# Windowed cross-attention on Trainium2: the projections of the next batch moved behind the attention of the older one

## What is computed

```python
def _L0_xattn_ref(x, cond, Wq, bq, Wk, bk, Wv, bv, Wo, bo):
    H, W = 8, 16                                  # heads, window
    q = Wq @ x + bq; k = Wk @ cond + bk; v = Wv @ cond + bv   # [128, 1024] per batch
    k, v = (pad(t, left=8, right=7) for t in (k, v))
    k_win, v_win = (t[:, :, arange(T)[:, None] + arange(W)[None, :]] for t in (k, v))
    dots = einsum('bhdt,bhdtw->bhtw', qh, k_win) * hd ** -0.5
    out = einsum('bhtw,bhdtw->bhdt', softmax(dots), v_win)
    return Wo @ out + bo
...
x = x + tanh(g_xattn[0]) * _L0_xattn_ref(_layernorm(x), ctx_4096, ...)
```

## Time and profile before

| what | value |
|---|---|
| median of 3 runs | 3655.55 us (3651.84 to 3661.02) |
| the profiled execution | 3649.41 us, span 3647.7 us |
| PE busy | 3294.2 us (90%) |
| DVE busy | 1433.3 us (39%) |
| ACT busy | 889.8 us (24%) |
| mean granted TensorE clock | 0.954 of full speed |

### The profile page before, as it was taken

The page is one execution under the profiler, slowest core; times in us unless marked ns, Lnnn a source line. Parts: engine busy times, 40 slices in busy tenths (PEclk is TensorE's granted clock), DMA queues, the critical chain, the costliest instruction groups (busy, mean ns, idle before and its releaser), DMA issues. The chain is left out here.

```text
span 3647.7 us, 52611 instructions
## 1 busy us (share of the span) xinstructions
PE 3294.2 (90%) x21047; PEld 2507.2 (69%) x21076; DVE 1433.3 (39%) x2021; ACT 889.8 (24%) x1232; POOL 349.3 (10%) x304
## 2 busy tenths in 40 slices
PE   5888855999799997899999669999999999999999
PEld 2454442777678885566666458888888888778777
DVE  6666657777220002677676362111121122310000
ACT  1222243333121112555454221111111111200000
POOL 2000000000000001232222111111111111000000
PEclk9999977999789998999999879999999999999999
DMA  4656451221232223121121243222222222544443
GB/s 95 131 115 126 89 185 35 70 70 59 76 104 69 61 60 110 70 85 58 64 80 63 66 131 103 91 94 94 94 94 94 94 94 82 202 145 132 141 141 104
DMA packets 339441, 352.61 MB, mean 97 GB/s; under 512 B 154352, under 2 KB 261472, under 8 KB 337264
## 3 DMA queue, kind: packets, MB, share of 16 engines
q1 hardware_dynamic: 339312, 350.79, 31.1%
HBM read 215.23 MB, written 126.97 MB: 94 GB/s over the span
## 5 line engine op out<-in xcount | busy, mean ns | idle before, releaser
L2213 PE MATMUL g_ps<-g_xs,g_wt 128*128 128x512 f32 x4128 | 957.2, 392 | 0.0
L2213 PEld LDWEIGHTS g_ps<-g_xs,g_wt 128*128 128x128 f32 x4128 | 774.3, 189 | 160.7
L2269 PE MATMUL g_ps<-g_wd,g_h 128*128 128x512 f32 x2016 | 463.0, 392 | 6.8 <-DMA g_h<-g_hidden 4.1
L2269 PEld LDWEIGHTS g_ps<-g_wd,g_h 128*128 128x128 f32 x2016 | 381.1, 189 | 88.1 <-DMA g_h<-g_hidden 4.7
L2131 DVE SCALAR_TENSOR_TENSOR g_act_out<-g_ps,g_g,g_act_out 128x512 f32<-128x512 f32 (+1 forms) x88 | 66.1, 751 | 691.4 <-ACT g_act_out L2063 691.4
L2063 ACT ACTIVATE g_act_out<-g_ps 128x512 f32<-128x512 f32 (+1 forms) x88 | 52.6, 598 | 655.7 <-PE g_ps L2213 655.7
L1263 PE MATMUL kv_gps<-kv_xh,kv_wh 128*128 128x512 f32 x512 | 200.5, 392 | 0.0
L1263 PE MATMUL kv_gps<-kv_xl,kv_wh 128*128 128x512 f32 x512 | 199.3, 389 | 0.0
L1263 PE MATMUL kv_gps<-kv_xh,kv_wl 128*128 128x512 f32 x512 | 199.3, 389 | 0.0
L1008 PE MATMUL f_gps<-f_xt,f_qwh 128*128 128x256 f32 x1024 | 194.2, 290 | 1.4 <-DVE f_xt L887 1.4
L1611 PEld LDWEIGHTS a_tps<-a_ident,a_e 128*128 128x128 f32 x1024 | 113.4, 144 | 104.6 <-issue 90.5
(11 more groups left out here) (247 smaller groups left out, 4257.6 us busy)
## 6 DMA issues: line engine op xcount, KB each, us to landing
g_h<-g_hidden SPq DMA_DIRECT2D x176, 256.0 KB, 2.6
g_hidden<-g_h SPq DMA_DIRECT2D x84, 512.0 KB, 2.7
kv<-kv_y SPq DMA_DIRECT2D x16, 1024.0 KB, 5.7
a_kv<-kv SPq DMA_DIRECT2D x16, 1024.0 KB, 4.9
g_xb<-x SPq DMA_DIRECT2D x24, 512.0 KB, 4.0
g_down<-g_raw SPq DMA_DIRECT2D x22, 512.0 KB, 2.8
g_raw<-g_down SPq DMA_DIRECT2D x22, 512.0 KB, 4.3
g_raw<-in_L_ffn_gate_w_dram SPq DMA_DIRECT2D x21, 512.0 KB, 4.0
```

The source lines that it names most:

```text
L2213: w = pe.matmul(gps[:, c % 2, m, :], wt[m][i][:, l, ks], xs[c][:, r, k, :], start=(k == 0 and a == 0), stop=(k == NK - 1 and a == 2))
L2269: w = pe.matmul(to, tile[:, p % RING, l, cols], wd[f][:, r, os], start=(f == 0 and a == 0), stop=False)
```

## The change

Five things are altered, in `window_attention` only.

1. x has five places instead of four, and its load is issued one batch earlier.
2. PE's order: the two key halves are projected first, alternating with `scores`; the attend loop has no values in it; the two query halves come between the last `attend` and the transposes of `output(b)`; the two value halves come between those transposes and the product with Wo, which is now `final(b)`.
3. The second half of the queries and of the values goes to a bank of the score ring instead of `prj` (`half_bank`), and the waits are changed to match.
4. ACT: keys first, queries after the last `middle`, the copy of `o` before the exponential. DVE: `normalize(b)` between the maximum and the subtraction, `value` halves around `sums`.
5. SP: `spread_keys` before `store_values`.

```diff
@@ -62,10 +62,11 @@
     RING = 3
+    XS = 5

         s = Scope(nc, ctx, "w")
-        x = s.sb("x", [P, 4, D])
+        x = s.sb("x", [P, XS, D])
         cond = s.sb("cond", [P, 2, D])
...
@@ -121,11 +122,15 @@

+        def half_bank(n, i, a):
+
+            return prj[:, :] if a == 0 or i == 1 else sps[:, (NK * n + i // 2) % RING, :]
+
         @block.sync
             def load_x(n):
-                past(sp, "res", n - 3)
-                sp.dma_start(x[:, n % 4, :], x_in[n]).then_inc(xl[n % 4], 16)
+                past(sp, "res", n - XS + 1)
+                sp.dma_start(x[:, n % XS, :], x_in[n]).then_inc(xl[n % XS], 16)

...
@@ -179,13 +185,13 @@
                     store(b - 1)
-                    if there(b + 3):
-                        load_x(b + 3)
+                    if there(b + 4):
+                        load_x(b + 4)
                 if b >= -1 and there(b + 3):
                 if there(b + 2):
+                    spread_keys(b + 2)
                     store_values(b + 2)
-                    spread_keys(b + 2)
                     spread_values(b + 2)
...
@@ -244,7 +250,7 @@
                 past(act, "s", NK * (n - 1))
-                act.activation(q[n % 2][:, 512 * a:512 * a + 512], prj[:, :], ACT.Identity, bias=bias[:, 0:1]).then_inc(S["sbq"], 1)
+                act.activation(q[n % 2][:, 512 * a:512 * a + 512], half_bank(n, 0, a), ACT.Identity, bias=bias[:, 0:1]).then_inc(S["sbq"], 1)

...
@@ -260,27 +266,28 @@
             for b in range(-2, B):
-                for i in range(4):
-                    if there(b + 2):
-                        (query, key)[i // 2](b + 2, i % 2)
+                for t in range(NK):
+                    if there(b + 2) and t < 2:
+                        key(b + 2, t)
                     if there(b + 1):
-                        middle(b + 1, i)
-                if there(b + 1):
-                    for t in range(4, NK):
                         middle(b + 1, t)
-                    act.wait_ge(S["sub"], b + 2)
-                    act.activation(sc[:, :, :, :], sc[:, :, :, :], ACT.Exp, scale=SCALE).then_inc(S["ex"], 1)
+                if there(b + 2):
+                    for a in range(2):
+                        query(b + 2, a)
                 if there(b):
                     act.copy(o[:, :], tps[:, :]).then_inc(S["oe"], 1)
+                if there(b + 1):
+                    act.wait_ge(S["sub"], b + 2)
+                    act.activation(sc[:, :, :, :], sc[:, :, :, :], ACT.Exp, scale=SCALE).then_inc(S["ex"], 1)

             def stats(n):
-                dve.wait_ge(xl[n % 4], 16 * (n // 4) + 16)
+                dve.wait_ge(xl[n % XS], 16 * (n // XS) + 16)
                 for c in range(2):
-                    dve.bn_stats(st[:, c, :], x[:, n % 4, 512 * c:512 * c + 512]).then_inc(S["stats"], 1)
+                    dve.bn_stats(st[:, c, :], x[:, n % XS, 512 * c:512 * c + 512]).then_inc(S["stats"], 1)
                 wait_apart(dve, S["c1"], (S["stats"], 2 * n + 2))
...
@@ -328,12 +335,14 @@
                 past(dve, "vst", 16 * n)
-                dve.tensor_tensor(vt[:, 4 * a:4 * a + 4, :], prj[:, :].rearrange("p (k c) -> p k c", c=P),
+                dve.tensor_tensor(vt[:, 4 * a:4 * a + 4, :], half_bank(n, 2, a).rearrange("p (k c) -> p k c", c=P),
                                   bvr[:, :].unsqueeze(1).to_broadcast([P, 4, P]), ALU.add).then_inc(S["sbv"], 1)

-            def shift(n):
+            def largest(n):
                 dve.wait_ge(S["sel"], NK * n + NK)
                 dve.tensor_reduce(mx[:, :], scu, AX.X, ALU.max).then_inc(S["mx"], 1)
+
+            def shift(n):
                 dve.wait_ge(S["mx"], n + 1)
...
@@ -363,16 +372,20 @@
                         select(b + 1, t)
-                    if there(b + 2) and t in (4, 7):
-                        value(b + 2, t // 7)
+                if there(b + 1):
+                    largest(b + 1)
+                if there(b):
+                    normalize(b)
                 if there(b + 1):
                     shift(b + 1)
-                if there(b):
-                    normalize(b)
                 if there(b + 3):
                     stats(b + 3)
+                if there(b + 2):
+                    value(b + 2, 0)
                 if there(b + 1):
                     sums(b + 1)
+                if there(b + 2):
+                    value(b + 2, 1)
                 if there(b + 3):
...
@@ -383,19 +396,19 @@
                 if i == 0:
-                    past(pe, "sbv", 2 * n) if a == 0 else pe.wait_ge(S["sbq"], 2 * n + 1)
+                    pe.wait_ge(S["sbk"], 2 * n + 2) if a == 0 else past(pe, "sel", NK * n - RING + 1)
                     pe.wait_ge(S["xn"], n + 1)
                 else:
-                    pe.wait_ge(S["sbq"], 2 * n + 2) if a == 0 else pe.wait_ge(S["sbk"], 2 * n + 1)
+                    past(pe, "sbv", 2 * n - 1) if a == 0 else pe.wait_ge(S["sbk"], 2 * n + 1)
                     pe.wait_ge(cl[n % 2], 16 * (n // 2) + 16)
                     src = cond[:, n % 2, 512 * a:512 * a + 512]
-                pe.matmul(prj[:, :], w4[:, i, :], src, start=True, stop=True).then_inc(S["pq" if i == 0 else "pk"], 1)
+                pe.matmul(half_bank(n, i, a), w4[:, i, :], src, start=True, stop=True).then_inc(S["pq" if i == 0 else "pk"], 1)

             def values(n, a):
-                pe.wait_ge(S["sbk"], 2 * n + 2) if a == 0 else pe.wait_ge(S["sbv"], 2 * n + 1)
+                pe.wait_ge(S["sbq"], 2 * n + 1) if a == 0 else past(pe, "sel", NK * n - RING + 2)
                 for k in range(4):
-                    m = pe.matmul(prj[:, P * k:P * k + P], cond[:, n % 2, P * (4 * a + k):P * (4 * a + k) + P], w4[:, 2, :],
+                    m = pe.matmul(half_bank(n, 2, a)[:, P * k:P * k + P], cond[:, n % 2, P * (4 * a + k):P * (4 * a + k) + P], w4[:, 2, :],
                                   start=True, stop=True)
...
@@ -403,6 +416,8 @@
                     pe.wait_ge(S["sbq"], 2 * n + 2)
+                if t == 1:
+                    pe.wait_ge(S["sbv"], 2 * n + 2)
                 i = NK * n + t
...
@@ -437,6 +452,8 @@
                 m.then_inc(S["ot"], 1)
+
+            def final(b):
                 pe.wait_ge(S["oe"], b + 1)
...
@@ -448,20 +465,27 @@
                     turn(b)
-                for i in range(4):
-                    if there(b + 2):
-                        project(b + 2, i // 2, i % 2)
-                    if there(b + 1) and i < 3:
-                        scores(b + 1, i)
+                for t in range(3):
+                    if there(b + 2) and t < 2:
+                        project(b + 2, 1, t)
+                    if there(b + 1):
+                        scores(b + 1, t)
                 for t in range(NK):
                         scores(b + 1, t + 3)
-                    if there(b + 2) and t in (1, 4):
-                        values(b + 2, t // 4)
+
+                if there(b + 2):
+                    for a in range(2):
+                        project(b + 2, 0, a)
                 if there(b):
                     output(b)
+                if there(b + 2):
+                    for a in range(2):
+                        values(b + 2, a)
+                if there(b):
+                    final(b)

```

More of the change, by code:

```diff
@@ L110, in window_attention @@
         S = {n: s.sem(n) for n in names}
-        xl = [s.sem(f"xl{i}") for i in range(4)]
+        xl = [s.sem(f"xl{i}") for i in range(XS)]
         cl = [s.sem(f"cl{i}") for i in range(2)]
@@ L171, in _ @@
             load_x(3)
+            load_x(4)
             sp.wait_ge(S["zp"], 1)
@@ L291, in norm @@
                 past(dve, "pq", 2 * n)
-                dve.tensor_scalar(xn[:, :], x[:, n % 4, :], mv[:, 0:1], rstd[:, 0:1], ALU.subtract, ALU.mult).then_inc(S["xn"], 1)
+                dve.tensor_scalar(xn[:, :], x[:, n % XS, :], mv[:, 0:1], rstd[:, 0:1], ALU.subtract, ALU.mult).then_inc(S["xn"], 1)
             stats(0)
@@ L356, in result @@
                 dve.scalar_tensor_tensor(out=y[:, :], in0=pvp[:, :], scalar=bias[:, 3:4],
-                                         in1=x[:, b % 4, :], op0=ALU.add, op1=ALU.add).then_inc(S["res"], 1)
+                                         in1=x[:, b % XS, :], op0=ALU.add, op1=ALU.add).then_inc(S["res"], 1)
             for b in range(-2, B):
```

## The result

The changed kernel took **3569.24 us** (median of 4 runs, 3566.53 to 3572.08), the kernel before 3656.47 (median of 4, 3651.84 to 3661.02): ratio 0.9762, 95% interval 0.9745 to 0.9778, that is 87 us less. The prediction was 3573, range 3560 to 3602.

A forecast was written before the change was run, and what follows sets the result against it. PE idling in dependent steps, with slow products behind, was taken to bound the stage; DVE would then pace it. 14 x (26.37 - 21.15) = 73.1, minus 1.5, plus 11.3, gave 82.9 us saved: 3573 us, range 3560 to 3602.

The forecast's parts named there:

- The period: Time of one steady iteration of the stage, `turn` to `turn`: 21.15 us, against 26.37 in the kernel before.
- The sum through DVE: Start-to-start steps of DVE and its partners from scores 7 to the next scores 7, a ring of 21.15 us.
- `sums` and the exponential meet without reserve: After scores 7, ACT's exponential ends near 7.7 us and DVE reaches `sums` at 7.69; any delay lengthens the period.
- PE alone: PE's own work in one iteration, if nothing else held it up: 20.35 us.
- The terms of its tail: PE's work at a batch's end: queries 1.82 us, transposes 1.09, value halves 1.1 each, product with Wo 1.82.
- The clock: PE's clock in the steady iterations: no half-speed stretch, so a fast 21.15 us replaces 26.37 with slow tails included.
- the other case: Rival: PE's clock still falls in the tails, at most 1.8 us a batch, 25 in all, 3598 us; chance 0.12.
- The store's landing: SP's wait for the values' store to land, 3.7 us, taken from SP's spare time, so not added to the period.
- the landing of a key copy: In SP's queue, 2.4 us for the last key copy to land, after 5.54 us of issues.
- in hand: Spare time between the last key copy's landing, at 20.9 us from `turn`, and the first scores at 23.0: 2.1 us.
- The fifth place: Fifth buffer place for x, keeping `stats` off the pinch in SP's queue; said to cost nothing.
- Beginning and end: First scores 8.7 us earlier plus 2.6 before `turn(0)`, together 11.3 gained; nothing taken for the last two iterations.

The follow-up runs named there:

- x5: Changed kernel with DVE's two statistics passes done twice, the second pair into a spare tile; 3592.68 us, single run.
- x6: Changed kernel with the second value half projected twice on PE; 3573.75 us, single run.
- x2: Changed kernel with DVE's subtraction of the maximum put ahead of `normalize` again; 3587.01 us, single run.
- x4: Changed kernel with all half projections sent through the one bank `prj` again; 3580.03 us, single run.
- x10: Changed kernel with DVE's first select between the two mask halves and `norm` behind select 4; 3553.03 us, 0.9727 of the kernel before.
- x9: Kernel before with useless matrix products put in PE's two holes, nothing else moved; 3638.57 us, single run.
- x3: Changed kernel with four places for x, each load issued one batch later; 3580.34 us, single run.
- x11: The changed kernel once more, not altered, timed against the kernel before on one chip; 3568.41 us, ratio 0.9763.
- x7: Changed kernel with DVE's first select put between the two halves of the masks; 3552.68 us, 0.9729 of the kernel before.
- x1: Changed kernel with SP storing the values before it spreads the keys, as in the kernel before; 3688.23 us, single run.

## Why the prediction was right, point by point

**The period.** Predicted 21.15, measured 21.03. The sum through DVE was right in kind (x5: DVE's extra time is paid nearly in full; x6: PE's is not) and in its terms: 1.20 to the last select, 4.00 from the masks to scores 3 (244.13 to 248.13), the wait of 0.99 before it (said: 0.8 to 1.1). The 0.12 us too much lie in the maximum, `normalize` and subtraction, which take 3.40 (234.20 to 237.60) and not 3.52. That `sums` and the exponential meet without reserve is right to 0.03 us, and x2 and x4, where the exponential comes later, show it: `sums` waits for it and the period grows. Fourteen periods gave 369.15 - 295.58 = 73.6 us, said 71.6.

**PE alone.** Said 20.35, it is 19.82 (x10). The terms of its tail were too large: the transposes occupy 0.87 until the next product (236.88 to 237.75) and not 1.09, their busy time, and a value half 0.9 and not the 1.1 taken from the projection. `turn` comes 8.92 after scores 7, not 9.5. Nothing hung on it, since PE was not the bound.

**The clock.** Taken as full, and 1.00 was granted. x9 measures what that was worth in the kernel before: 1.18 us a batch, 19.4 for the stage. x5 and x3 show how near the other case lay: DVE 1.2 us later was enough. Its chance of 0.12 was not too high.

**SP.** The store's landing was not paid, as taken: in the changed kernel SP stood 39.4 us for it, but also 45.4 us for the value halves, and ahead of the keys it still stood for the last scores, 5.6 us in ten batches. It came early, then, and had the time to spare. The Trainium skill's rule ("DMA: Bandwidth & Descriptors", "Rules for kernel authors") would have that landing hidden; here the trace shows the wait that it describes, but in time that SP had to spare. The term that was mis-sized is the landing of a key copy: 2.4 was taken from the kernel before, where the copies followed the store of the values, and it is 3.7 behind the result's store and the loads. A second error met it. The prediction let the last copy be issued when all issues are over, 5.54 after the first; it is issued 4.35 after it, since the 5.54 take in the last issue itself, whose landing counts from its beginning. The last copy of the period shown, which began at 237.62:

```profile
L155 SPq DMA_DIRECT2D w_kbd<-w_kp x1: 1742/1742/1742, 237.6 to 237.6; - x1
...
DMA to landing us min/median/max: 3.6/3.6/3.6
```

It landed at 241.24, 7.97 after the first issue, where the prediction had 7.94 from two wrong terms. The scores came at 243.08: 1.84 in hand, said 2.1. That the sum came out is luck, and not every batch is like this one: from 75 us on there was 0.6 to 2.4 in hand, and in x11 one batch had nothing left, though its period was still 21.03. With shorter periods, four batches of x7 and five of x10 had nothing left.

**The fifth place.** "It costs nothing" stands; it is worth 9.4 us of the stage by x3, 3.5 of them through the clock, which the prediction did not give it.

**Beginning and end.** First scores at 37.09 (said 38.1), `turn(0)` 13.5 us earlier (said 11.3: the first scores are 1.0 earlier than said, and the time from them to `turn(0)` shrank by 3.7 and not 2.6). From `turn(14)` to the next stage it took 0.8 more than before. In all the stage gave 86.2 us where 82.9 were said; the rest of the program took 3.3 more in this execution, which is less than it varies by itself, and so the profiled total agrees with the sum to 0.1 by luck.

## What to carry to other kernels

Work that depends on nothing recent belongs in the holes between dependent steps. Here it filled the holes and the clock stayed up, and even useless products there gave 19 us. When such a move is made, list for each engine and each queue what waits behind the moved step: here a swap of two issues decided between 87 us won and a loss of 37. Then close the ring with start-to-start distances, not busy times, and take a transfer's landing at its new place in the queue, where it was half as long again here.

## What was not expected of the hardware

Behind two waits of PE, 2.1 us apart, the granted clock went to 1.2 GHz in some batches and not in others, at a price of 1.7 us each. With waits of 0.68 and 1.25 us it fell in five of x5's batches and stayed up in eight; with 0.80 and 1.25 and with 1.47 and 1.25 it fell in x3; one wait of 0.99 never did it in the 13 batches of the changed kernel.

Eight copies of 65 KB landed in 2.4 us in the median straight behind a 512 KB store of the values (kernel before, and 2.4 in x1 too), but in 3.7 behind the store of the result and the loads of x and cond together, and in 2.9 behind the load of cond, with the other two issued after them. So it is not the presence of 512 KB ahead that makes them late. What in the loads does it was not separated.

The later stages, the same code each time, took 3172.0 to 3182.5 us in 14 profiles.
